# Fourth tile of a threshold sum on VectorE, the logits' means read later, and the LayerNorm blocks in another order

## What is computed

```python
for n in range(STEPS):                       # STEPS = 2
    A = _top_p_attention(Xa, W1, W2, W3)     # 2048 x 2048, softmax, nucleus of 0.9
    Xf = R @ Xf
    Xa = A @ Xa
    Z = Z + Xf @ U1[n].T + Xa @ U2[n].T
h = X + Z                                    # then a LayerNorm with gain and bias
# outer: x = x + h ; h = relu(layernorm(x)) ; the third layer starts with incidence.T @ h
```

## Time and profile before

| what | value |
|---|---|
| three runs | 1132.78, 1136.21, 1137.52 us, median 1136.21 us |
| the profiled execution, its own time | 1135.15 us |
| its span, first to last instruction | 1133.4 us |
| TensorE busy | 839.8 us (74%) |
| VectorE busy | 766.4 us (68%) |
| ScalarE busy | 508.6 us (45%) |
| GpSimd busy | 69.2 us (6%) |
| granted TensorE clock, mean | 0.883 of full speed |

### The profile page before, as it was taken

The page is one execution under the profiler, slowest core; times in us unless marked ns, Lnnn a source line. Parts: engine busy times, 40 slices in busy tenths (PEclk is TensorE's granted clock), DMA queues, the critical chain, the costliest instruction groups (busy, mean ns, idle before and its releaser), DMA issues.

```text
span 1133.4 us, 12143 instructions
## 1 busy us (share of the span) xinstructions
PE 839.8 (74%) x3886; PEld 566.2 (50%) x3886; DVE 766.4 (68%) x2271; ACT 508.6 (45%) x972; POOL 69.2 (6%) x65
## 2 busy tenths in 40 slices
PE   5789968844786768659778177678568999995496
PEld 5744325622655656555455055557466484552142
DVE  5968689879959969932897797798686302323533
ACT  4876231365476486224213835935946241123011
POOL 0120110000000000000000000000031000003111
PEclk9889979876998989979788589989879999997698
DMA  9869013210022022000134000400340657300000
GB/s 343 308 237 413 19 74 129 99 70 2 1 75 75 1 74 75 1 1 1 40 109 148 1 1 1 149 1 1 112 156 24 252 245 297 149 1 1 1 10 28
DMA packets 18731, 105.48 MB, mean 93 GB/s; under 512 B 1744, under 2 KB 7392, under 8 KB 8416
## 3 DMA queue, kind: packets, MB, share of 16 engines
q1 hardware_dynamic: 17264, 104.02, 24.7%
q10 hardware_dynamic: 1392, 0.61, 0.2%
HBM read 85.74 MB, written 18.88 MB: 92 GB/s over the span
## 4 chain that ended last, share of the span: by engine, by line
PE 37%; DVE 29%; issue 15%; ACT 14%; POOL 2%; DMA 1%; DVEq 1%; POOLq 0%; SPq 0%; ACTq 0%
DVE AT L1419 12%; PE PS L740 8%; PE PS L611 5%; PE PS L985 5%; ACT BC L1168 5%; PE PS L678 5%; ACT AT L1168 4%; DVE mxv L1557 4%; PE PS L481 4%; PE PS L798 3%; DVE nd L1422 3%; PE PS L547 2%; DVE se L1412 1%; DVE AT L1977 1%; ACT AT L1001 1%
## 5 line engine op out<-in xcount | busy, mean ns | idle before, releaser
L678 PE MATMUL PS<-K,ST 128*128 128x512 f32 x224 | 127.3, 721 | 90.7 <-ACT EA L1136 66.3
L1001 ACT ACTIVATE AT<-PS 128x512 f32<-128x512 f32 (+2 forms) x240 | 118.5, 558 | 131.9 <-PE PS L481 117.8
L678 PEld LDWEIGHTS PS<-K,ST 128*128 128x128 f32 x224 | 49.7, 234 | 153.3 <-issue 153.2
L481 PE MATMUL PS<-ident,AT 128*128 128x128 f32 x544 | 82.5, 285 | 49.1 <-DVE rS L2017 24.2
L1419 DVE SCALAR_TENSOR_TENSOR AT<-EA,se 128x2048 uint8<-128x2048 f32 (+1 forms) x50 | 116.8, 2345 | 1.1 <-PE PS L481 0.2
L481 PEld LDWEIGHTS PS<-ident,AT 128*128 128x128 f32 x544 | 66.2, 147 | 57.8 <-ACT AT L1001 26.2
L1419 DVE SCALAR_TENSOR_TENSOR AT<-AT 128x2048 uint8<-128x2048 f32 (+2 forms) x44 | 86.7, 1971 | 11.1 <-PE PS L481 10.2
L1557 DVE TENSOR_REDUCE mxv<-PS 128x1 f32<-128x2048 f32 x32 | 73.1, 2285 | 23.5 <-PE PS L678 18.0
L1977 DVE MAX8 AT<-AT 128x8 f32<-128x256 f32 x256 | 88.4, 412 | 0.8
L1001 ACT ACTIVATE ST<-PS 128x512 f32<-128x512 f32 (+3 forms) x43 | 24.0, 560 | 127.7 <-PE PS L985 36.2
L740 PE MATMUL PS<-AT 128*128 128x128 f32 x512 | 70.1, 287 | 13.0 <-ACT AT L1001 12.6
(11 more groups left out here) (287 smaller groups left out, 1423.2 us busy)
## 6 DMA issues: line engine op xcount, KB each, us to landing
AT<-keep_at SPq DMA_DIRECT2D x32, 1024.0 KB, 5.1
EA<-in_adj SPq DMA_DIRECT2D x28, 1024.0 KB, 6.5
keep_at<-AT SPq DMA_DIRECT2D x8, 2048.0 KB, 24.9
AT<-keep_at SPq DMA_DIRECT2D x7, 2048.0 KB, 12.9
AT<-in_adj SPq DMA_DIRECT2D x4, 1024.0 KB, 10.0
EA<-keep_degrees SPq DMA_DIRECT2D x1, 1024.0 KB, 6.4
keep_x<-K SPq DMA_DIRECT2D x4, 256.0 KB, 6.8
out<-EA SPq DMA_DIRECT2D x4, 256.0 KB, 2.3
```

Of the source, the lines that this page charges most:

```text
L481: return pe.transpose(dst, src, ident[0:p, 0:p])
L678: mm = pe.matmul(bank(half(gi, k) + n), ST[1][:, k * P:(k + 1) * P], wide_keys[:, n * BK:(n + 1) * BK], start=True, stop=True)
L1001: return act.activation(dst, src, ACT.Copy)
```

## The change

It has three parts.

1. `sums_below(..., 0, ...)` on ScalarE does tiles 0, 1 and 2 and leaves out tile 3. VectorE does tile 3 in `last_tile`, a `mass_above` behind `doubtful`, and puts its result in by `last_surplus`, one small instruction behind `surplus_below`. `surplus_below` waits for six sums and no longer for eight. The array `below` is cleared once at the start.
2. `logit_mean(gi + 2)` stands behind the list rounds, ahead of `crossing_checked`.
3. The LayerNorm blocks: behind the tiles of group 6 only block 0 is done, both halves at once; block 1 and block 2 move behind them, in between `multiplied(0)` to `multiplied(4)`. `LN_ORDER` finishes block 0 first.

```diff
-        LN_ORDER = ((0, 0), (1, 0), (0, 1), (1, 1), (2, 0), (2, 1))
+        LN_ORDER = ((0, 0), (0, 1), (1, 0), (1, 1), (2, 0), (2, 1))
...
             def blocks_ahead(k):
 
-                if k > 0:
-                    rows_summed((k - 1) // 2, (k - 1) % 2)
-                rows_turned(k // 2, k % 2)
+                for h in range(2):
+                    if k == 1:
+                        rows_turned(0, h)
+                    elif k == 2:
+                        rows_summed(0, h)
...
-            rows_summed(1, 1)
-            pe.wait_ge(ln_x2, 2 * G)
-            for t in range(G):
-                multiplied(t)
-            for h in range(2):
-                rows_turned(2, h)
-                rows_summed(2, h)
-            for t in range(G, 2 * G + 2):
-                multiplied(t)
+            def both(part, b):
+
+                for h in range(2):
+                    part(b, h)
+
+            multiplied(0)
+            multiplied(1)
+            both(rows_turned, 1)
+            multiplied(2)
+            both(rows_summed, 1)
+            multiplied(3)
+            both(rows_turned, 2)
+            multiplied(4)
+            both(rows_summed, 2)
+            for t in range(5, 2 * G + 2):
+                multiplied(t)
...
                 if k == 0:
                     first_scaled(0)
+                elif k == 1:
                     turned_out(0, 0)
-                    first_norm(1)
-                elif k == 1:
+                    turned_out(0, 1)
+                elif k == 2:
                     summed_out(0, 0)
-                    turned_out(0, 1)
-                    first_scaled(1)
-                elif k == 2:
                     summed_out(0, 1)
-                    turned_out(1, 0)
                     second_norm(0)
                 else:
-                    summed_out(1, 0)
-                    turned_out(1, 1)
                     second_scaled(0)
...
                     if more:
-                        sums_below(step, g + 1, 0, (0, 1, 2, 3))
+                        sums_below(step, g + 1, 0, (0, 1, 2))
...
                 else:
+                    first_norm(1)
+                    first_scaled(1)
+                    turned_out(1, 0)
+                    turned_out(1, 1)
+                    summed_out(1, 0)
                     summed_out(1, 1)
                     second_norm(1)
                     first_norm(2)
                     second_scaled(1)
                     first_scaled(2)
...
+            v.put(dve.memset(below[:, :, :], 0.0))
...
-                dve.wait_ge(sum_ok, sums_by(gi, m) + 2 * (G - m))
+                dve.wait_ge(sum_ok, sums_by(gi, m) + 2 * (G - 1))
...
+            def last_tile(q, gi):
+
+                mass_above(EA if gi % 2 == 0 else EB, gi, G - 1)
+                v.wait()
+
+            def last_surplus(q):
+
+                v(tt(q.fval[:, G - 1:G], Fv[:, G - 1:G], q.Tt[:, G - 1:G], ALU.subtract))
...
-                if left > 1:
-                    logit_mean(gi + 2)
                 v.wait()
                 v.put(total(seen8, tops[0][:, :, TOP - 1:SETS * TOP:TOP], ALU.max))
...
+                if left > 1:
+                    logit_mean(gi + 2)
                 crossing_checked(q)
                 doubtful()
                 if left > 0:
+                    last_tile(nq, gi + 1)
                     surplus_below(nq, gi + 1, 0)
+                    last_surplus(nq)
                     first_step(nq)
```

More of the change, by code:

```diff
@@ L280, in turned_at @@
         def turned_at(b, h):
-            return bank(h if b < 2 else 4 + h)
+            return bank(h if b == 0 else 4 + h)
         def summed_at(b, h):
-            return bank(2 + h if b < 2 else 6 + h)
+            return bank(2 + h if b == 0 else 6 + h)
         def normed_at(b, second):
@@ L302, in sums_by @@
         def sums_by(gi, m=0):
-            return 2 * ((2 * G - 1) * (gi - gi // NB - 1) + G * m)
+            return 2 * (G - 1) * (2 * (gi - gi // NB - 1) + m)
         block = ctx.enter_context(nc.Block())
@@ L765, in rows_turned @@
                 pe.wait_ge(ln_y, G * (b + 1))
-                if b == 1:
-                    pe.wait_ge(ln_ts, h + 1)
+                if b == 2:
+                    pe.wait_ge(ln_ts, 2 + h + 1)
                 for k in range(2):
@@ L779, in rows_summed @@
                 elif b == 1:
-                    pe.wait_ge(ln_x2, 2 * (h + 1))
+                    pe.wait_ge(z_ok, NT + RING)
                 else:
-                    pe.wait_ge(z_ok, NT + RING)
+                    pe.wait_ge(ln_x2, G + 2 * (h + 1))
                 for k in range(2):
@@ L1336, in _ @@
                     first_scaled(2)
-                    for h in range(2):
-                        turned_out(2, h)
-                        summed_out(2, h)
+                    turned_out(2, 0)
+                    turned_out(2, 1)
+                    summed_out(2, 0)
+                    summed_out(2, 1)
                     second_norm(2)
@@ L2020, in group @@
                     v(tt(num, num, pa, ALU.add))
-                    mass_above(EB if gi % 2 == 0 else EA, gi + 1, G - 1)
-                    v.wait()
+                    last_tile(nq, gi + 1)
                     surplus_below(nq, gi + 1, 1)
-                    v(tt(nq.fval[:, G - 1:G], Fv[:, G - 1:G], nq.Tt[:, G - 1:G], ALU.subtract))
+                    last_surplus(nq)
                     next_step(nq, 0)
```

## The result

The changed kernel takes **1118.26 us** (median of 4 runs, 1116.85 to 1120.26), the kernel before 1136.87 us beside it: ratio 0.9839, 95% interval 0.9817 to 0.9861. Forecast were 1116 us and a range of 1110 to 1123. The profiled execution took 1117.8 us of its own time with a span of 1116.0, where before it was 1135.15 and 1133.4; by these two the change gave 17.4 us.

What follows compares the result with a forecast made beforehand. No engine holds half the chain, so handovers were taken to bound the kernel. Middle 21.1 less tail 1.4 gave 19.7 us off 1135.15, 1115.4; forecast 1116 us (median-based 1116.5), own range 1112.5 to 1119.5, wider range 1110 to 1123.

Steps and rivals of the forecast that it cites:

- The middle: Six first threshold sums, with the later means read, less `last_surplus`, plus gi = 2's second sum: 21.1 us gained.
- The new release is the later of the two: First sum: ScalarE ready 3.97 us earlier, VectorE s + m - 2.44 (waits for sum and means); the later engine sets the release.
- ScalarE's wait for the unit: In gi = 1 and 5 ScalarE, done with six sums, waits some 2.1 us for TensorE's unit; 1 us lost on ScalarE.
- the cover of the second sum: VectorE needs the second sum only at 353.1, ScalarE has it about 351.2, so the 1 us lost costs nothing.
- The means: Read moved behind the list rounds, to about 324.3 instead of 322.5 in gi = 1: no cost, gain counted in m.
- The tail: Reordered LayerNorm blocks up to `attend` of group 7: 0.4 us gained, 1.8 lost to the clock; costs 1.4, bounds 0 to 4.
- ScalarE's chain from block 1's last sums to the end of `first_scaled(2)`: Tail: takes 7.4 us as before, so block 2's rows come late.
- the stall ahead of block 2's transposes: Tail: TensorE waits from 881.7 to 886.3 for `first_scaled(2)`, some 4.6 us.
- what the clock costs behind it: After TensorE's 4.6 us stall the clock falls to its lower rate: 1.8 us.
- one `multiplied` takes 3.46 us: Tail, TensorE: each `multiplied` lasts 3.46 us, so `multiplied(1)` ends at 871.55 after a start at 864.65.
- nothing in that chain is changed: Tail: ScalarE's way from block 1's last sums to the end of `first_scaled(2)` keeps its earlier 7.4 us.
- the tail is worse: Rival: GpSimd's roots last longer and the clock falls in other TensorE gaps too; 4 us more, 1119.5 us; chance 0.12.

Runs made afterwards that it cites:

- h_after: The changed kernel run once more, same program, in the third set: 1120.55 us, ratio 0.9834 to the kernel before.
- c_nomean: Changed kernel with the means read ahead of the list rounds again: 1125.17 us, ratio 0.9915 to the kernel before.
- f_fill: Changed kernel with 18 unused transposes of the identity on TensorE ahead of `multiplied(0)`: 1118.48 us, ratio 0.982 to the kernel before.
- g_both: e_norm with block 2's sums ahead of `multiplied(4)` on TensorE and its copies ahead of `second_scaled(1)` on ScalarE: 1113.0 us, ratio 0.9774.
- a_middle: Changed kernel with the LayerNorm blocks in the old order, keeping the new first sum and means: 1113.21 us, ratio 0.981 to the kernel before.
- i_two: Changed kernel with one more tile of the first sum moved, so VectorE scans tiles 2 and 3: 1132.3 us, ratio 0.9946.
- e_norm: Changed kernel with block 2's first norm and scaling on ScalarE ahead of its wait for block 1's sums: 1118.81 us, ratio 0.9818.
- k_both: g_both run once more, same program, in the third set: 1112.67 us, ratio 0.9769 to the kernel before.
- g_best: g_both and f_fill together: 1116.11 us, ratio 0.9802 to the kernel before.

## Why the prediction was right, and where it was off

**The middle**: forecast 21.1 us, in the profile 22.7. "The new release is the later of the two" is confirmed place by place: VectorE's waits were to be about 2.7 us in gi = 1 and 5 and none in gi = 0, 2 and 6, and were 2.65, 3.10 and none; in gi = 4, for which only an average with gi = 5 was taken, it was 0.43. The groups gave 3.0, 3.8, 2.9 with 0.4 for gi = 2's second sum in 2-3, 4.2, 3.8 and 4.7 us. The last is off by 1.7 us: before, VectorE waited 2.58 us there for logits at the lower clock (the row of 5.37 us), in the changed kernel 0.93; this is the clock's chance and not the change's merit, as h_after shows, the same program as the changed kernel, where this wait was 2.58 us again and the group took 79.8 us. The others are within 0.4 us. Step 0 got 10.1 us shorter where some 10 were forecast, and step 1 12.7 where some 11 were, 1.7 of them by this chance. ScalarE's wait for the unit was 1.91 us (forecast 2.1), and the cover of the second sum held: ScalarE had it at about 347.7, VectorE's own scan of it ended at 349.7, without a wait.

**The means**: as forecast, moved at no cost. Undone alone (c_nomean) it costs its 1.05 us in gi = 1 and 0.8 in gi = 5, and 5 us elsewhere that the means don't explain. That the same edit on the kernel before gives a ratio below 1 was not forecast, and its cause is open.

**The tail is the term that was mis-sized**: forecast to cost 1.4 us, measured 5.7. Three of its parts were as forecast: ScalarE's chain from block 1's last sums to the end of `first_scaled(2)` (7.4, measured 7.40 from 859.65 to 867.05), the stall ahead of block 2's transposes (4.6, measured 4.58) and what the clock costs behind it (1.8, measured 2.1: from 868.01 to 876.30 it was 8.29 us, where 3.46 + 2.7 were due). What failed is the step "one `multiplied` takes 3.46 us" for the first two. They start behind 2.08 us of idle time, and `multiplied(0)` ran at the lower clock: 10.0 us for both from 842.39 to 852.37, where 6.9 were forecast, 3.1 more. That the gap brought the slow products is shown by f_fill. Everything behind, and ScalarE's copies of block 1 with it, came that much later. `multiplied(0)` itself gained 6.1 us and not 6.9, 0.8 more. With 0.1 ahead of the stall and 0.3 behind it, 1.4 + 3.1 + 0.8 + 0.1 + 0.3 = 5.7 us.

This sum says where the time of this execution went, and not what each term would give back. In f_fill the 3.1 us are gone, and `attend` of group 7 starts only 0.3 us earlier: block 1's root then fell into VectorE's masking scans, and the chain of 7.4 us took 10.05. So "nothing in that chain is changed" was the weaker step. With the first two `multiplied` as fast as forecast, as they are in f_fill, the tail still loses 5.4 us. And g_both gained its 6.9 us with the slow products in place. What the new order costs is the late work of block 2 on ScalarE.

I had the rival "the tail is worse", with 4 us more by roots that last longer and by other falls of the clock, at 0.12, and that is what happened. The forecast's nearness is in part luck: in the profiled executions the time is 2.4 us above the sum of 1115.4, with 4.3 us more lost in the tail than forecast and 1.7 us of chance won in the middle.

**The fastest of all kernels run here** is g_both (0.9774 and 0.9769): parts 1 and 2 as changed, and block 2's work on ScalarE ahead of the wait for block 1.

## What to carry to other kernels

Where two engines work towards one release, take from each how much earlier it would be there, and move work only up to the point where they are equal: with one tile moved and the means read later (a_middle) the kernel gained 1.9%, a second tile (i_two against h_after) cost 1.1%. An order in which the results come earlier is worth nothing when the engine that feeds the next step gets its work in the old order: follow each block to its last consumer. Before a gap is filled, look at what waits behind it: the filled gap of f_fill gave 3 us at one place, and a wait for another engine took 2.5 of it. The length of a chain, taken from one trace, holds only while the chain meets the same neighbours.

## What the runs showed of the hardware

**The clock fell behind a short gap.** Behind an idle time of 2.08 us the next products ran at a clock of 0.50; in the 4 us ahead TensorE had been busy for 1.49 us in small pieces. With the gap filled (f_fill) the clock was 1.00. Before the change, the gap ahead of `multiplied(0)` was 0.71 us and the four products ran at full clock, in 14.00 us. The Trainium skill, "TensorE: Matmul & The Clock Gate", section "HAM oscillation — how this bites in real kernels", ties the fall to a gap that is long enough. By the length of the gap alone these rows can't be told apart: 2.08 us of idle brought the fall here, and 3.05 us did not (below). The same eight logits took 3.67 us behind 3.05 us of idle in the changed kernel and 5.37 us behind 2.00 us in c_nomean.

**Equal code meets another clock from one execution to the next.** The same eight logits L678 of group 5-6, in the changed kernel and then in e_norm, which has the same code there:

```profile
737.29 3.67 PE L678 MATMUL PS<-K,ST 128*128 128x512 f32 x8 [3.05 <-ACT AT L1145]
```

```profile
738.14 5.37 PE L678 MATMUL PS<-K,ST 128*128 128x512 f32 x8 [3.35 <-ACT AT L1145]
```

In the kernels with the middle of the changed one, groups 0-1, 1-2, 4-5 and 5-6 of the table take one of two values, 1.6 to 3.3 us apart, with the same instructions; the changed kernel itself, run twice (changed, h_after), took 76.4 and 79.8 us in 5-6. So one profile tells a difference of 3 us only if the group's rows are looked at, and the median of the kernel before was 3.3 us apart between two sets.

**GpSimd's small instructions wait for VectorE's scan to end.** L448 takes 0.19 us by itself. It took 0.43, 1.19 and 2.00 us when it began inside a 128x2048 scan of VectorE (L1419, now L1429), and ended each time 0.05 us behind the end of that scan. k_both, with 2.00 us, and VectorE's scan:

```profile
863.02 2.00 POOL L448 TENSOR_SCALAR nd<-nd 128x4 f32<-128x4 f32 x1 [12.52 <-ACT ST L1222]
...
862.62 2.35 DVE L1429 SCALAR_TENSOR_TENSOR AT<-AT,s 128x2048 f32<-128x2048 f32 x1
```

L450, 1.01 us by itself, took 3.00 us in f_fill and g_best and ended 0.86 us behind a scan's end; in the kernel before it did so too, at block 0 (2.98 us from 827.88). Over all profiles of this case, 26 of these two instructions began inside such a scan, and all 26 ended 0.05 us (L448) or 0.87 us (L450) behind it, while the other 142 took at most 0.23 and 1.06 us. The Trainium skill, "SBUF — State Buffer", section "SBUF: two separate sides", has a rule for it: VectorE and GpSimd share one pair of ports as an exclusive lock, which a VectorE instruction with two inputs in SBUF holds to its end against a GpSimd instruction that reads SBUF. The scans have two such inputs (`stt` is given `E` twice), and the rows agree. No run here gave the scan one input, so the rows show that the scan's end releases the root, and not that the ports are the reason.
